# Cross attention over each batch's own 64 keys, in the two column halves of the array, with a reworked loading phase

## The reference, cut to what matters

```
x = x + self_attention(layernorm(x))      # 16 heads of 16, causal, ALiBi bias, within a batch
x = x + cross_attention(layernorm(x), ctx, mask)
x = x + ffn(layernorm(x))                 # 256 -> 1024 -> 256, weights rounded to MXFP4, gelu
# cross_attention, one head of 256, within a batch:
scores = (h @ ctx.T) / 16; scores = where(mask, scores, -1e30)    # 64 tokens x 64 keys
out = softmax(scores) @ ctx; out = 0 where a batch has no unmasked key
```

## Time and profile before

| | us |
|---|---|
| median of 3 runs (lowest, highest) | 143.77 (143.28, 144.34) |
| the profiled execution, whole time | 142.73 |
| its span in the trace | 140.9 |
| PE busy | 117.4 (83%) |
| DVE busy | 109.8 (78%) |
| ACT busy | 94.8 (67%) |
| POOL busy | 61.9 (44%) |

### The profile page before, as it was taken

The page is one execution under the profiler, slowest core; times in us unless marked ns, Lnnn a source line. Parts: engine busy times, 40 slices in busy tenths (PEclk is TensorE's granted clock), DMA queues, the critical chain, the costliest instruction groups (busy, mean ns, idle before and its releaser), DMA issues.

```text
span 140.9 us, 3182 instructions
## 1 busy us (share of the span) xinstructions
PE 117.4 (83%) x1046; PEld 84.5 (60%) x1046; DVE 109.8 (78%) x253; ACT 94.8 (67%) x212; POOL 61.9 (44%) x108
## 2 busy tenths in 40 slices
PE   0035999869898997998999899798999679999991
PEld 0014743627634466775767678567787259899970
DVE  0758489999999999999999999977664595664642
ACT  2123347656776776667668876679995699999970
POOL 7565349305450045446477884526543085000000
PEclk9999999999999999999999999999999999999999
DMA  4899999970000000000000000000000200020202
GB/s 144 269 348 329 368 302 334 353 239 1 2 5 0 2 0 5 0 0 0 5 0 7 0 0 0 5 0 2 5 0 0 74 0 0 5 77 0 81 0 74
DMA packets 8864, 10.70 MB, mean 76 GB/s; under 512 B 1648, under 2 KB 7920, under 8 KB 8720
## 3 DMA queue, kind: packets, MB, share of 16 engines
q1 hardware_dynamic: 7760, 9.64, 21.1%
q10 hardware_dynamic: 1088, 0.86, 2.0%
HBM read 9.45 MB, written 1.05 MB: 74 GB/s over the span
## 4 chain that ended last, share of the span: by engine, by line
PE 40%; DVE 26%; issue 11%; DMA 11%; ACT 4%; POOL 4%; SPq 1%; DVEq 1%; ACTq 0%
PE bank L1100 10%; PE bank L1116 10%; DMA x_sb<-in_x_dram 6%; DMA raw_T<-in_W_down_T_dram 4%; DVE s_sb L805 4%; DVE s_max L810 4%; DVE k L781 3%; PE bank L1023 3%; PE bank L958 3%; PE bank L983 3%; PE bank L1050 2%; PE bank L1039 2%; DVE stats L758 2%; PE bank L971 2%; POOL rstd L560 2%
## 5 line engine op out<-in xcount | busy, mean ns | idle before, releaser
L592 POOL TENSOR_TENSOR s_sb<-s_sb,s_max 128x512 f32<-128x512 f32 x16 | 18.0, 1127 | 25.8 <-DVE s_max L810 25.8
L928 DVE TENSOR_TENSOR h_lo<-h_sb,h_hi 128x256 fp32r<-128x256 f32 x32 | 14.2, 442 | 10.9 <-ACT h_sb L726 10.7
L958 PE MATMUL bank<-const,xn 128*128 128x128 f32 x48 | 11.0, 319 | 12.9 <-DVE xn L767 10.8
L1100 PE MATMUL bank<-xn_T,w_up_q 128*128 128x256 f16 x128 | 19.4, 274 | 0.7 <-ACT h_sb L726 0.7
L1116 PE MATMUL bank<-w_down_q,h_hi 128*128 128x256 f32 x64 | 18.9, 320 | 0.5 <-DVE h_lo L928 0.2
L726 ACT ACTIVATE h_hi<-bank,bias_cols 128x256 fp32r<-128x256 f32 x32 | 15.4, 481 | 1.9 <-issue 0.4
L1116 PE MATMUL bank<-w_down_q,h_lo 128*128 128x256 f32 x64 | 16.5, 281 | 0.0
L560 POOL TENSOR_TENSOR rstd<-var_eps,minus_half 128x1 f32<-128x1 f32 x24 | 14.8, 617 | 2.0
L958 PEld LDWEIGHTS bank<-const,xn 128*128 128x128 f32 x48 | 5.9, 155 | 16.2 <-issue 8.9
L726 ACT ACTIVATE h_sb<-bank,bias_cols 128x256 f32<-128x256 f32 x32 | 15.4, 481 | 0.0
L971 PE MATMUL bank<-xn_T,w_T 128*128 128x512 f32 x32 | 15.1, 611 | 0.1
(11 more groups left out here) (86 smaller groups left out, 265.2 us busy)
## 6 DMA issues: line engine op xcount, KB each, us to landing
raw_T<-in_W_up_T_dram SPq DMA_DIRECT2D x1, 1024.0 KB, 10.3
raw<-in_W_up_dram SPq DMA_DIRECT2D x1, 1024.0 KB, 12.7
ctx_T<-in_ctx_by_feature_dram SPq DMA_DIRECT2D x1, 1024.0 KB, 7.1
ctx_sb<-in_ctx_dram SPq DMA_DIRECT2D x1, 1024.0 KB, 9.4
raw_T<-in_W_down_T_dram SPq DMA_DIRECT2D x1, 1024.0 KB, 6.3
raw<-in_W_down_dram SPq DMA_DIRECT2D x1, 1024.0 KB, 8.3
out_dram<-x_sb SPq DMA_DIRECT2D x8, 128.0 KB, 1.8
x_sb<-in_x_dram SPq DMA_DIRECT2D x4, 128.0 KB, 3.6
```

The costliest lines, as they stand in the source:

```text
L592: pool.tensor_tensor(tile, tile, s_max[:, u % S_RING, :].unsqueeze(2).broadcast_to([P, HC, S]), ALU.subtract).then_inc(centred, 1)
L928: dve.tensor_tensor(h_lo[:, i % H_RING, :], h_sb[:, i % GELU_RING, :], h_hi[:, i % H_RING, :].bitcast(F32), ALU.subtract).then_inc(split_r ...
L958: last = pe.transpose(dst[:, c * P:(c + 1) * P], xn[:, ring[t % len(ring)], c * P:(c + 1) * P], ident)
L1100: last = pe.matmul(dst[:, 0:GN], w_up_q[:, c, f * P:(f + 1) * P], xn_T16[:, g * GT:(g + 1) * GT, at16:at16 + P], start=(k == 0), stop=(k = ...
```

## The change

Cross attention is done per batch. `x_scores` issues, for each of the two feature chunks, two matmuls with 64 stationary columns and 64 moving columns, one per batch, whose results land in the two partition halves; the scores are 128 x 64. The mask matmul, the maximum, the exponential and the transpose work on 64 columns. The transposed probabilities are 64 x 128 (`xp_T`), the context lies by tokens on 64 partitions (`ctx_sb` is 64 x 16 x 256, not 128 x 8 x 256), and `x_read` is two matmuls, one per batch. The factor `valid` (0 for a batch without keys) moves from `x_prob_copy` on ACT into `x_scale` on DVE, which becomes two instructions with a wait between them.

In the loading phase SP waits for `W_qk` where it waited for `W_v`, so that `alibi` and all behind it are issued later; DVE zeroes its half of `v2` before the first statistics; `x_mask` is half as large. `stages()` gets other assumed durations, `schedule()` a rule that lengthens some DVE stages when POOL streams at the same time, and all numbers of `URGENCY`, `DRIFT` and `PATIENCE` are new (for example `amax` 8 to 60, `k_rest` 19 to -77, `x_scores` 22 to -26, patience of DVE 0.1 to 0.16). The order of the stages on every engine can so differ anywhere.

```diff
--- before.py
+++ after.py
@@ -46,7 +46,6 @@
-OTHER_ROW = -2e30
...
@@ -77,24 +76,26 @@
     def layer_norm(n, t, before):
...
-        add("stats", (n, t), "dve", 0.55, before)
-        add("rstd", (n, t), "pool", 1.1 if n in NORM_ON_ACT else 0.85, [("stats", (n, t))])
+        add("stats", (n, t), "dve", 0.55, before + ([("v2_zero2", ())] if n == LN1 else []))
+        add("rstd", (n, t), "pool", 1.18 if n in NORM_ON_ACT else 0.85, [("stats", (n, t))])
...
-        add("norm", (n, t), "act" if n in NORM_ON_ACT else "dve", 0.28 if n in NORM_ON_ACT else 0.32, [("rstd", (n, t))] + reused)
+        add("norm", (n, t), "act" if n in NORM_ON_ACT else "dve", 0.49 if n in NORM_ON_ACT else 0.32, [("rstd", (n, t))] + reused)
...
-    loads = (("load_x", (0,), 2.0), ("load_x", (1,), 0.4), ("load_x", (2,), 0.4), ("load_x", (3,), 0.4),
-             ("load_v", (), 0.9), ("load_x", (HALF,), 1.5), ("load_biases", (), 0.1), ("load_qk", (), 1.5),
-             ("load_alibi", (), 1.5), ("load_rows", (), 0.4), ("load_blocks", (), 3.0), ("load_weights", (), 3.0),
-             ("load_row_biases", (), 0.8), ("load_o", (), 0.8), ("load_mask", (), 0.3), ("load_ctx", (), 6.0))
+    loads = (("load_x", (0,), 2.0), ("load_x", (1,), 0.2), ("load_x", (2,), 0.2), ("load_x", (3,), 0.2),
+             ("load_v", (), 0.8), ("load_x", (HALF,), 1.4), ("load_biases", (), 0.1), ("load_qk", (), 1.3),
+             ("load_alibi", (), 2.3), ("load_rows", (), 0.2), ("load_blocks", (), 2.8), ("load_weights", (), 2.8),
+             ("load_row_biases", (), 0.6), ("load_o", (), 0.6), ("load_mask", (), 0.1), ("load_ctx", (), 5.8))
...
+    add("v2_zero", (), "pool", 2.5)
+    add("v2_zero2", (), "dve", 1.6)
...
@@ -116,10 +117,9 @@
-            add("v_even", (h, pair), "act", 0.49, [("v", (h, pair)), ("v2_zero", (h,))])
-            add("v_odd", (h, pair), "dve", 0.6, [("v", (h, pair)), ("v2_zero", (h,))])
-        add("v2_zero", (h,), ("pool", "dve")[h], 2.5)
-    add("x_fill", (), "pool", 1.4)
+            add("v_even", (h, pair), "act", 0.49, [("v", (h, pair)), (("v2_zero", "v2_zero2")[h], ())])
+            add("v_odd", (h, pair), "dve", 0.6, [("v", (h, pair)), (("v2_zero", "v2_zero2")[h], ())])
+    add("x_fill", (), "pool", 1.0)
...
@@ -148,18 +148,18 @@
-        add("x_scores", (t,), "pe", 0.6, [("turn_copy", (LN2, t)), ("load_ctx", ()), ("x_table", ())], [7], ("x_exp", (t,)))
-        add("x_max", (t,), "dve", 0.24, [("x_scores", (t,))])
+        add("x_scores", (t,), "pe", 0.4, [("turn_copy", (LN2, t)), ("load_ctx", ()), ("x_table", ())], [7], ("x_exp", (t,)))
+        add("x_max", (t,), "dve", 0.15, [("x_scores", (t,))])
...
-        add("x_exp", (t,), "act", 0.4, [("x_max", (t,))] + reused)
+        add("x_exp", (t,), "act", 0.33, [("x_max", (t,))] + reused)
...
-        add("x_prob_copy", (t,), "act", 0.18, [("x_prob_T", (t,)), ("valid", ())] + ([("x_read", (t - 2,))] if t >= 2 else []))
-        add("x_scale", (t,), "dve", 0.1, [("x_exp", (t,))])
-        add("x_read", (t,), "pe", 0.47, [("x_prob_copy", (t,))], [5], ("x2", (t,)))
+        add("x_prob_copy", (t,), "act", 0.28, [("x_prob_T", (t,))] + ([("x_read", (t - 2,))] if t >= 2 else []))
+        add("x_scale", (t,), "dve", 0.22, [("x_exp", (t,)), ("valid", ())])
+        add("x_read", (t,), "pe", 0.5, [("x_prob_copy", (t,))], [5], ("x2", (t,)))
...
-    add("x_table", (), "dve", 0.9, [("x_fill", ()), ("load_mask", ())])
+    add("x_table", (), "dve", 1.0, [("x_fill", ()), ("load_mask", ())])
...
@@ -193,13 +193,13 @@
-            add("up", (i,), "pe", 0.4, lows + [("q_out", (UP, 1))], [i % 2], ("gelu", (i,)))
+            add("up", (i,), "pe", 0.37, lows + [("q_out", (UP, 1))], [i % 2], ("gelu", (i,)))
...
-            add("down", (i,), "pe", 0.53, [("split", (i,)), ("q_out", (DOWN, 1))], banks, ("final", (tiles[-1],)))
+            add("down", (i,), "pe", 0.56, [("split", (i,)), ("q_out", (DOWN, 1))], banks, ("final", (tiles[-1],)))
...
@@ -210,40 +210,45 @@
+STREAMS = ("centre", "add_bo", "add_down", "v2_zero", "x_fill", "max", "round")
+TWO_PORT = ("norm", "k_rest", "binade", "q_cut", "q_inverse", "q_exponent", "q_step", "q_clip", "x_table")
+STRETCH = 1.1
...
 URGENCY = {
...
 DRIFT = {
...
 PATIENCE = {
...
@@ -281,6 +286,7 @@
+    streaming = 0.0
...
@@ -297,6 +303,10 @@
+        if engine == "dve" and key[0] in TWO_PORT and streaming > start:
+            us += min(STRETCH * us, 0.6 * (streaming - start))
+        if engine == "pool" and key[0] in STREAMS:
+            streaming = start + us
...
@@ -336,7 +346,7 @@
-        ctx_sb = sb("ctx_sb", [P, TILES, E])
+        ctx_sb = sb("ctx_sb", [S, B, E])
...
@@ -351,7 +361,7 @@
-        x_mask = sb("x_mask", [S, TILES, P], BF16)
+        x_mask = sb("x_mask", [S, TILES, S], BF16)
...
@@ -377,11 +387,12 @@
-        xs_sb = sb("xs_sb", [P, 2, P])
+        xs_sb = sb("xs_sb", [P, 2, S])
...
-        xp_T = sb("xp_T", [P, 2, P])
+        xs_scale = sb("xs_scale", [P, TILES])
+        xp_T = sb("xp_T", [S, 2, P])
...
@@ -502,7 +513,7 @@
-            sp.wait_ge(v_loaded, 16)
+            sp.wait_ge(qk_loaded, 16)
...
@@ -519,7 +530,7 @@
-            sp.dma_start(ctx_sb[:, :, :], ctx.rearrange("(t b) s e -> (b s) t e", b=2)).then_inc(ctx_loaded, 16)
+            sp.dma_start(ctx_sb[:, :, :], ctx.rearrange("b s e -> s b e")).then_inc(ctx_loaded, 16)
...
                 if stage == "reload":
...
@@ -563,14 +574,14 @@
-                if stage == "v2_zero" and at[0] == 0:
+                if stage == "v2_zero":
...
                 if stage == "x_fill":
-                    pool.memset(x_mask[:, :, :], OTHER_ROW).then_inc(x_mask_filled, 1)
+                    pool.memset(x_mask[:, :, :], 0.0).then_inc(x_mask_filled, 1)
...
                     for b in range(2):
@@ -680,7 +691,7 @@
-                    act.activation(xs_sb[:, t % 2, :], bank[7][:, 0:P], ACT.Exp, bias=xs_negmax[:, t:t + 1],
+                    act.activation(xs_sb[:, t % 2, :], bank[7][:, 0:S], ACT.Exp, bias=xs_negmax[:, t:t + 1],
...
                 if stage == "x_prob_copy":
...
@@ -688,9 +699,7 @@
-                    act.wait_ge(valid_ready, 1)
-                    act.activation(xp_T[:, t % 2, :], bank[6][:, 0:P], ACT.Identity,
-                                   scale=valid[:, t:t + 1]).then_inc(x_probs_copied, 1)
+                    act.activation(xp_T[:, t % 2, :], bank[6][0:S, 0:P], ACT.Copy).then_inc(x_probs_copied, 1)
                 if stage == "scale_copy":
...
@@ -782,7 +791,7 @@
-                if stage == "v2_zero" and at[0] == 1:
+                if stage == "v2_zero2":
...
@@ -834,7 +843,7 @@
                     for b in range(2):
...
-                        dve.tensor_scalar(x_mask[row, :, b * S:(b + 1) * S], mask_rows_u8[row, :, :], -MASKED,
+                        dve.tensor_scalar(x_mask[row, :, :], mask_rows_u8[row, :, :], -MASKED,
...
                 if stage == "valid":
...
@@ -842,17 +851,20 @@
                 if stage == "x_max":
...
-                    dve.tensor_reduce(xs_negmax[:, t:t + 1], bank[7][:, 0:P], AX_X, ALU.max,
+                    dve.tensor_reduce(xs_negmax[:, t:t + 1], bank[7][:, 0:S], AX_X, ALU.max,
...
                 if stage == "x_scale":
...
-                    dve.reciprocal(xs_inv[:, t:t + 1], xs_sum[:, t:t + 1]).then_inc(x_scale_ready, 1)
+                    dve.wait_ge(valid_ready, 1)
+                    step(dve.reciprocal(xs_inv[:, t:t + 1], xs_sum[:, t:t + 1]))
+                    dve.tensor_tensor(xs_scale[:, t:t + 1], xs_inv[:, t:t + 1], valid[:, t:t + 1],
+                                      ALU.mult).then_inc(x_scale_ready, 1)
                 if stage == "x2":
...
-                    dve.scalar_tensor_tensor(out=x_sb[:, t, :], in0=bank[5][:, 0:E], scalar=xs_inv[:, t:t + 1],
+                    dve.scalar_tensor_tensor(out=x_sb[:, t, :], in0=bank[5][:, 0:E], scalar=xs_scale[:, t:t + 1],
...
                 if stage == "amax":
...
@@ -1047,21 +1059,25 @@
-                        pe.matmul(dst[:, 0:P], xn_T[:, t, c * P:(c + 1) * P], ctx_T[:, t, c, :],
-                                  start=(c == 0), stop=False)
-                    pe.matmul(dst[:, 0:P], x_own[:, :], x_mask[:, t, :], start=False, stop=True).then_inc(
+                        for b in range(2):
+                            tok = slice(c * P + b * S, c * P + (b + 1) * S)
+                            pe.matmul(dst[b * S:(b + 1) * S, 0:S], xn_T[:, t, tok], ctx_T[:, t, c, b * S:(b + 1) * S],
+                                      start=(c == 0), stop=False)
+                    pe.matmul(dst[:, 0:S], x_own[:, :], x_mask[:, t, :], start=False, stop=True).then_inc(
...
                 if stage == "x_prob_T":
...
-                    pe.transpose(dst[:, 0:P], xs_sb[:, t % 2, :], ident).then_inc(x_probs_turned, 1)
+                    pe.transpose(dst[0:S, 0:P], xs_sb[:, t % 2, :], ident).then_inc(x_probs_turned, 1)
                 if stage == "x_read":
...
```

(13 more changed lines are left out.)

37 lines of the change are left out of this document (15 added, 22 removed).

## The result

The kernel became slower: 150.69 us (median of 4 runs, 150.36 to 152.25) against 143.53 us (4 runs) for the kernel before on the same chip, a ratio of 1.0573 with the interval 1.0509 to 1.0636. Executions of one kernel spread by some per cent (in this comparison 141.5 to 144.3 us for the kernel before), so each ratio here is taken over the faster executions of both kernels, and where the median of all executions tells something else, it stands beside it; here it is 1.050. The profiled execution took 152.25 us, its span is 150.5 us, and its mean granted clock is 0.932 where that of before was 1.000. PE is busy 121.7 us (before 117.4), DVE 108.1 (109.8), ACT 93.1 (94.8), POOL 64.1 (61.9).

The account below looks back on a forecast made before the run. Loading waits for data, then DVE is full, then PE and DVE, and PE at the end. 142.73 - 2.8 + 1.5 - 1.4 - 0.3 + 0.5 = 140.2 us profiled, 141.3 as a median, given as 141.0; range 137.0 to 144.9.

Parts of the forecast that it names:

- the loss at the down weights: DVE's `amax` of the late down weights takes back 1.5 us of the 2.8 gained in loading, bounds 0 and 4.8.
- D: Rival: `ctx_sb` loads onto 64 partitions at half rate, 6.0 not 3.0 us, with C's wait: 147.6 us, chance 0.10.
- C: Rival: down-weights `amax` keeps its place and ends 2.0 us later, cross attention gives 1.2: 144.6 us, chance 0.14.
- the gain of the cross attention: Cross attention stages on PE, ACT and DVE: -1.4 - 0.3 + 0.5, a gain of 1.2 us.
- `W_qk` is there at 8.3 us: Loading: x and `W_qk` land at 8.3 us, x's second half 2.8 us sooner, bounds 1.5 to 3.5.
- Every later byte arrives up to 2.0 us later: Loads queued behind SP's wait: `alibi` issued at about 8.4 us, not 4.49; shift 2.0 us, bounds 0 to 2.5.
- The fills: Loading: DVE zeroes `v2` while idle for the first tile, beside POOL's fill; cost zero, uncovered up to 1.7 us.
- `x_scores`: Cross attention scores on PE: 0.39 us instead of 0.64, saving 0.25 a tile, bounds 0.15 to 0.35.
- `x_read`: Cross attention read on PE: 0.49 us instead of 0.43, a cost of 0.06 a tile, bounds -0.17 to +0.63.
- Rival E: Column halves don't help on PE: `x_scores` 0.49 and `x_read` 1.06 us, 146.5 us in all, chance 0.05.
- ACT and DVE: Cross attention: cheaper copy and exponential on ACT, -0.3 us; second `x_scale` instruction less shorter `x_max` on DVE, +0.5 us.
- The new order: Changed order of stages on all engines: 0 us, with 2 us either way.

Follow-up runs that it names:

- `before_wait_qk`: The kernel before with only SP's wait changed, to `W_qk` instead of `W_v` ahead of `alibi`: ratio 1.0271.
- `after_ctx128`: The changed kernel with the context by tokens loaded onto 128 partitions; odd batches read the even batch's context, matmul count and shape kept: ratio 1.0182.
- `after_told`: The changed kernel with its planner told 13 us for each reload, not 5, so four pairs of `add` and `max` precede the first down-weights `amax`: 1.0735.
- `before_quad`: The kernel before with the new cross attention on two diagonal quarters of the array, context kept on 128 partitions: ratio 1.0013.
- `after_quad_v`: The changed kernel with cross attention on diagonal quarters, context on 128 partitions, and SP waiting for `W_v` again: ratio 0.9967.
- `after_warm`: The changed kernel with seven extra unused matmuls on PE where it waits in the first 50 us: ratio 1.0454, by the median of all four executions 1.059.
- `after_wait_v`: The changed kernel with SP waiting for `W_v` as before instead of `W_qk`: ratio 1.0393, by the medians of all executions 1.047.
- `before_xattn_late`: The kernel before with the new cross attention alone, its 64-partition `ctx_sb` load issued behind both down-weight reloads: ratio 1.0117.
- `before_xattn`: The kernel before with the new cross attention alone, including the 64-partition `ctx_sb` load; order, SP's wait and fills kept: median 150.41 us, ratio 1.0466.

## Why the prediction was wrong

Forecast 141.0 us with a range of 137.0 to 144.9; it is 150.7. Two steps of the sum failed: the load of `ctx_sb` onto 64 partitions had no term in it and costs 3.5 to 3.9%, 5.0 to 5.6 us; and the loss at the down weights was put at 1.5 of the 2.8 us gained, where SP's wait by itself made the kernel 2.7% slower. Both reach the end through the `amax` of the down weights. The rival that came true is D together with C, given 0.10, and it was priced 3.1 us too low (147.6). About 1.2 of these are the gain of the cross attention, which D still counted and which didn't come; the other 2.1 are the `amax`, at 36.26 us where D has 34.2 (C's 31.2 and 3.0).

- **The step that failed first: D held for a side case, its load put at nothing.** The prediction gave the load onto 64 partitions no place in its sum, since no load of the trace wrote so few. Measured: 191 to 216 GB/s against 365 to 401 for loads onto 128, with the DMAs' busy share over 1 in both. By 210 and 375 GB/s its 1.05 MB take 5.0 us and not 2.8. D had 3.0 us for it, and 2.8 were counted from 26 to 32 us. D's size for the load was right. The Trainium skill (SBUF — State Buffer, Door 1: The DMA port swizzle) states that partitions 0 to 63 reach half of the ports, with 196 GB/s against 328 for 1 MiB. The trace agrees: 191 to 216 on the low figure, and more than the page has on the high one. D was given 0.10 for lack of a row, and the lack of a row was no evidence against it.
- **"`W_qk` is there at 8.3 us."** It landed at 10.54 in after and by 8.77 in `before_wait_qk`. By 8.2 us after had moved 159 GB/s x 4.4 us (a window not shown), 223 x 1.7 (likewise) and 297 x 2.1, together 1.70 MB of the 1.91. That is 0.17 MB less than was counted from the trace of before, and the last 0.21 MB took 2.4 us at 86 GB/s and a DMA share of 0.25. The step took the queue's rate to the last byte; in this execution the last bytes ran at a quarter of it. It isn't always so: `alibi`, which goes out when `W_qk` has landed, went out at 7.0 to 10.6 us in seven profiles, and 8.3 lies in between. The gain at x's second half was 0.4 us in after and 2.0 in `before_wait_qk`, 0.6 on the mean of all profiles, not 2.8.
- **"Every later byte arrives up to 2.0 us later."** This held. In `before_wait_qk` `alibi` went out 4.3 us later (3.9 were forecast) and the `amax` of the down weights started at 31.21 us, in `after_ctx128` at 31.31; C has 31.2. In after `alibi` went out 6.1 us later, and 121 GB/s from 10.6 to 13.0 us show the queue refilling.
- **The loss of 1.5 of the 2.8 us at the down weights** (bounds 0 to 4.8). DVE's idle time there was 6.89 us, and 4.59 with SP's wait alone. Even with the upper bound the two terms (-2.8 + 4.8) come to 2.0 us slower; `before_wait_qk`, which has them alone, is 3.9 us slower than the kernel before by the medians (146.37 against 142.44). The forecast hoped for `add` and `max` ahead of the wait; the order had none there, and `after_told`, which has them, was slower still. The place was right: the prediction named this wait and said that it would be wrong if the wait were longer than 3 us.
- **The fills.** DVE's ran from 1.25 to 3.12 us beside POOL's (1.99, 1.92 us): no disturbance, as predicted.
- **`x_scores`** 0.38 us against 0.39 predicted; **`x_read`** 0.58 against 0.49, inside its bounds. Rival E is out. Summed by group, `x_scores` went from 5.3 to 3.6 us and `x_read` stayed at 5.2 us. That is not the 1.4 us off the path that the sum took: `before_quad` has these matmuls, with quarters in `x_read`, and gains nothing (1.0013, by its interval between 0.5 us faster and 0.9 slower).
- **ACT and DVE:** Copy 263 ns (275 predicted), exponential 308 against 362, `x_max` 216 (220 predicted), `x_scale`'s second instruction 160 (158). All right, and all too small to count.
- **The new order, 0 with 2 us either way:** 0.9967 [0.993, 1.0005] in `after_quad_v` bears this out.
- **Not in the sum at all:** the clock. With PE short of work from 26 us on it ran at 1.2 GHz from 36 to 52 us. What that cost isn't settled: 1.7 us by the ratio of `after_warm`, whose four executions are 3.9 us apart.

The change's parts, shown by themselves: the layout on 64 partitions +4.5% in the kernel before (1.0466 to 1.0013), SP's wait +1.8 to +2.7% (three pairs, of which that of `after_wait_v` is only 0.3% by the medians), the rest nothing. In the changed kernel they come off one after the other: 1.0573, 1.0185 with the context on 128 partitions, 0.9967 with SP's old wait as well. That is 3.9 and 2.2%, the whole loss.

What stays open: the 1.2% of `before_xattn_late`; why `before_xattn` lost 6.7 us for an `amax` 3.2 us late; which stage of `after_told`'s order starves PE; and the clock's share.
